# Last combining of the routed layer: VectorE held until the last result writes are issued, ScalarE scales half of the first choices

## The chip, the cores and the metric

The kernel runs on one core of one Trainium2 chip. The metric is the device time of one execution in microseconds (us); lower is better.

## The reference

Four layers follow each other on an activation x of 4 batches x 1024 positions x 128 features, each as x = x + layer(layernorm(x)): linear attention with decay, a mixture of 8 experts, a state-space layer, and a second mixture of experts ("routed"). Only the last one's end is touched here. Cut to what matters:

```python
combine, dispatch = _top2_gating(x @ router_w, capacity)        # 8 experts, two choices for each token
expert_in  = einsum('nec,nh->ech', dispatch, x)
hmid       = silu(einsum('ech,ehf->ecf', expert_in, w1) + b1)
expert_out = einsum('ecf,efh->ech', hmid, w2) + b2
y   = einsum('nec,ech->nh', combine, expert_out)               # w_a * first choice + w_b * second choice
out = y + 0.1 * (silu(x @ sw1 + sb1) @ sw2 + sb2)
x   = x + out
```

## The kernel before, in words

Each engine has its own instruction stream; they wait for each other through semaphores. The 4096 tokens lie in SBUF as 8 chunks of 128 partitions x (4 batches x 128 features) in `xs`. The last phase, `routed_phase`, sorts the tokens into expert queues in device memory (`queue_in`) and works through 40 groups of 256 queue rows: SP loads a group (line 1245), TensorE turns it, multiplies by W1 (L1387) and W2 (L1399), ScalarE applies the gate (L1464), and VectorE adds the second bias into `outs` (`kept_of`, L1616).

GpSimd writes each group back to `results` in device memory, in the order of the tokens, with two indirect DMAs of 128 rows (L1306): 80 in all, each taking its row numbers from `target` in SBUF. Three groups may be in flight. Before issuing group t, and three times after the loop, GpSimd runs `all_landed` (L1279 to L1282): it waits until group t - 3 has landed and raises the semaphore `sent` with `pool.sem_inc` (L1282).

`results` has a half for the first choices and a half for the second ones. The expert queues hold the first choices ahead of the second ones, so SP can load the first half into `back[0]` (the buffer `XN`, L1251) before the loop over the groups is done: it waits for a number of groups computed from the data (L1249). The second half is loaded into `back[1]` (the buffer `XT`, L1256) only after all 40 groups have landed (L1252); chunk 4 to 7 of it wait for the landing of the chunk four before.

The last combining is `xs += w_a * back[0]` and then `xs += w_b * back[1]`, chunk by chunk:

- VectorE adds the first choices of all 8 chunks, four instructions a chunk, one for each batch because the weight is one number a partition and batch (`weighted`, L1634 to L1643). They are `scalar_tensor_tensor` on 128x128 (L1637), 32 in all; the last of each chunk raises `weighed`. They come right after the last `kept_of` in VectorE's stream and wait only for `first_in`.
- VectorE then adds the second choices of chunks 0, 2, 4 and 6 the same way (L1644 to L1647).
- ScalarE scales the second choices of chunks 1, 3, 5 and 7 in place (L1469 to L1474), and GpSimd adds them to `xs` in one 128x512 `tensor_tensor` a chunk (L1318), once `weighed` says that the chunk's first choices are in. These stand in GpSimd's stream behind the last `all_landed`.
- SP stores the chunks 0 to 7 in this order (L1259).

Of the kernel before, what the change touches and what calls it, by code (L numbers as in the profile page):

```python
# [8 lines left out]
ALU = mybir.AluOpType  # L9
ACT = mybir.ActivationFunctionType  # L10
AX = mybir.AxisListType

P = 128
BATCH, SEQ, D = 4, 1024, 128
CHUNKS = SEQ // P
WIDE = BATCH * P
# [11 lines left out]
def at(i, per_turn, k):  # L28

    return i * per_turn + k  # L30


def wide(ap, n=BATCH):
    return ap.rearrange("p (b f) -> p b f", b=n)
# [1137 lines left out]
def routed_phase(nc, xs, of, queue_in, results, out, routing, w1, w2, b1, b2, sw1, sw2, sb1, sb2):  # L1172
# [3 lines left out]
    with ExitStack() as ctx:  # L1176
# [17 lines left out]
        best, second, w_a, w_b = (S.sb(n, TILES) for n in ("best", "second", "w_a", "w_b"))  # L1194
# [12 lines left out]
        back = [XN, XT]  # L1207
# [3 lines left out]
        s = {n: S.sem(n) for n in ("spread shared_in late_in columns kept lg_mm lg_out chain expd exped masked prefix slots "  # L1211
                                   "s_hid s_act s_outp s_evac due dispatched sent "
                                   "e_turned e_cols rows_read e_hid e_act e_outp e_outs weighed scaled "
                                   "first_in combined combined_pool stored").split()}
        fetched = [S.sem(f"fetched{k}") for k in range(4)]
        written = [S.sem(f"written{k}") for k in range(IN_FLIGHT)]

# [44 lines left out]
        @block.gpsimd  # L1262
        def _(pool):
            front.inverse_deviation(pool)
            pool.memset(restart[:, :], 1.0).then_inc(s["spread"], 1)
            pool.wait_ge(s["spread"], 1)
            pool.memset(restart[:, :].rearrange("p (k n) -> p k n", n=TILES)[:, :, 0:1], 0.0).then_inc(s["spread"], 1)
            with pool.Fori(0, CHUNKS // 2) as i:
                for k in range(2):
                    pool.wait_ge(front.normal, at(i, 2, k + 1))  # L1270
                    pool.sem_inc(front.held, 1)
                    pool.tensor_copy(by_row(XN[:, bass.ds(i * 2 * BATCH * ROW + k * BATCH * ROW, BATCH * ROW)])[:, :, 0:D],
                                     wide(front.xn[k][:, :])).then_inc(s["kept"], 1)

            pool.wait_ge(s["kept"], CHUNKS)
            pool.wait_ge(s["slots"], 2)
            landed = [0] * IN_FLIGHT

            def all_landed(k, what):  # L1279

                pool.wait_ge(written[k], landed[k])
                pool.sem_inc(what, 1)  # L1282

            n = 0
            for choice in range(2):
                for b in range(BATCH):
                    for c in range(CHUNKS):
                        tile = c * BATCH + b
                        if n >= IN_FLIGHT:
                            all_landed(n % IN_FLIGHT, s["dispatched"])  # L1290
                        pool.indirect_dma_start(queue_in, bass.IndirectOffsetOnAxis(slot[:, n:n + 1], 0),  # L1291
                                                XN[:, tile * ROW:(tile + 1) * ROW], None,
                                                bounds_check=SLOTS - 1, oob_is_err=False
                                                ).then_inc(written[n % IN_FLIGHT], 16)
                        landed[n % IN_FLIGHT] += 16
                        n += 1
            for n in range(SCATTERS, SCATTERS + IN_FLIGHT):
                all_landed(n % IN_FLIGHT, s["dispatched"])

            for t in range(GROUPS_OUT):  # L1300
                if t >= IN_FLIGHT:
                    all_landed(t % IN_FLIGHT, s["sent"])
                pool.wait_ge(s["e_outs"], t + 1)
                for j in range(2):
                    n = t % KEPT_BACK * 2 + j
                    pool.indirect_dma_start(results, bass.IndirectOffsetOnAxis(target[:, n:n + 1], 0),  # L1306
                                            outs[t % KEPT_BACK][:, j * P:(j + 1) * P], None,
                                            bounds_check=2 * BATCH * SEQ - 1, oob_is_err=False
                                            ).then_inc(written[t % IN_FLIGHT], 16)
                landed[t % IN_FLIGHT] += 32  # L1310
            for t in range(GROUPS_OUT, GROUPS_OUT + IN_FLIGHT):
                all_landed(t % IN_FLIGHT, s["sent"])

            for c in range(1, CHUNKS, 2):
                xc_ = xs[:, c * WIDE:(c + 1) * WIDE]
                pool.wait_ge(s["scaled"], c // 2 + 1)
                pool.wait_ge(s["weighed"], c + 1)
                pool.tensor_tensor(xc_, xc_, back[1][:, c * WIDE:(c + 1) * WIDE], ALU.add).then_inc(s["combined_pool"], 1)  # L1318
# [104 lines left out]
        @block.scalar  # L1423
        def _(act):
            act.sem_inc(s["lg_mm"], 2)
            with act.Fori(0, CHUNKS // 2) as i:
                for k in range(2):
                    act.wait_ge(front.turned, at(i, 2, k + 1))
                    act.activation(XT[:, bass.ds(i * 2 * WIDE + k * WIDE, WIDE)], front.turn[k][:, :], ACT.Copy)
                    act.wait_ge(s["lg_mm"], at(i, 2, k + 1))  # L1430
                    act.activation(xc[k][:, :], front.turn[k][:, :], ACT.Copy).then_inc(s["columns"], 1)
            act.wait_ge(s["expd"], 1)
            act.activation(logits[:, :], logits[:, :], ACT.Exp).then_inc(s["exped"], 1)

            def shared_gate(c):
                for m in range(HB):
                    act.wait_ge(s["s_hid"], c * HB + m + 1)
                    act.activation(hT[c % 2][:, m * WIDE:(m + 1) * WIDE], banks[m][:, :], ACT.Silu,
                                   bias=SB1[:, m:m + 1]).then_inc(s["s_act"], 1)

            def shared_kept(c):
                act.wait_ge(s["s_outp"], c + 1)
                act.activation(shared[:, c * WIDE:(c + 1) * WIDE], outp[c % 2][:, :], ACT.Copy).then_inc(s["s_evac"], 1)  # L1443

            act.wait_ge(s["shared_in"], 16 * len(shared_loads))
            shared_gate(0)
            shared_kept(0)
            shared_gate(1)
            for c in range(1, CHUNKS):
                if c + 1 < CHUNKS:  # L1450
                    act.wait_ge(s["s_outp"], c)
                    shared_gate(c + 1)
                shared_kept(c)

            act.wait_ge(s["late_in"], 16 * len(late))
            for t in range(GROUPS_OUT):
                e = t % EXPERTS
                if t >= 2:
                    act.wait_ge(s["e_outp"], t - 1)
                for h in range(HB // 2):  # L1460
                    q = t * HB // 2 + h
                    act.wait_ge(s["e_hid"], q + 1)
                    for m in (2 * h, 2 * h + 1):
                        last = act.activation(hT[t % 2][:, m * GROUP:(m + 1) * GROUP],  # L1464
                                              banks[q % 4][:, (m % 2) * GROUP:(m % 2 + 1) * GROUP], ACT.Silu,
                                              bias=B1[:, e * HB + m:e * HB + m + 1])
                    last.then_inc(s["e_act"], 1)

            for c in range(1, CHUNKS, 2):  # L1469
                act.wait_ge(*second_in[c])  # L1470
                for b in range(BATCH):
                    yb = back[1][:, c * WIDE + b * P:c * WIDE + (b + 1) * P]
                    last = act.activation(yb, yb, ACT.Copy, scale=w_b[:, b * CHUNKS + c:b * CHUNKS + c + 1])
                last.then_inc(s["scaled"], 1)  # L1474

        @block.vector
        def _(dve):
# [156 lines left out]
            def weighted(back_, w, c):  # L1634
                for b in range(BATCH):
                    xb = xs[:, c * WIDE + b * P:c * WIDE + (b + 1) * P]
                    last = dve.scalar_tensor_tensor(xb, back_[:, c * WIDE + b * P:c * WIDE + (b + 1) * P],  # L1637
                                                    w[:, b * CHUNKS + c:b * CHUNKS + c + 1], xb, ALU.mult, ALU.add)
                return last

            dve.wait_ge(s["first_in"], 16 * CHUNKS)
            for c in range(CHUNKS):
                weighted(back[0], w_a, c).then_inc(s["weighed"], 1)  # L1643
            for c in range(0, CHUNKS, 2):  # L1644
                dve.wait_ge(*second_in[c])
# [739 lines left out]
```

## Time and profile before

| | us |
|---|---|
| median of the 3 runs | 1039.56 (1039.24 to 1043.19) |
| the profiled execution's own time | 1034.82 |
| its span in the trace | 1033.0 |
| TensorE busy | 881.3 |
| VectorE busy | 551.8 |
| GpSimd busy | 480.9 |
| ScalarE busy | 444.4 |

Times in the trace are from the span's start. Engines: PE is TensorE, DVE is VectorE, ACT is ScalarE, POOL is GpSimd, SP is SyncE, which only issues DMAs. A name with a q (POOLq, SPq) is the engine's sequencer, which decodes the stream and hands instructions on to the engine. L12 is line 12 of the kernel. The chain of work is followed back from the last instruction through whatever released each step.

### The profile page before, as it was taken

What the parts mean: (1) busy time and instruction counts of PE and PEld (TensorE: products, weight loads), DVE (VectorE), ACT (ScalarE), POOL (GpSimd) and SP (SyncE); (2) the same over time, 40 slices, a digit from 0 to 9 for tenths busy, and PEclk for the clock granted to TensorE, in tenths of its full rate; (3) what the DMA queues carried; (4) which work ended last, traced back from release to release, by engine and by line L of the source; (5) the groups of instructions that cost most, each with busy time, mean ns of one, the idle gap of its engine ahead of it and who ended that gap; (6) DMA issues with size and microseconds to landing.
All of it is one profiled execution on the core that took longest, in us unless ns stands there. A gap on an engine that the chain in (4) does not pass through costs nothing. (4 is left out here: it accounts for less than half of the span.)

```text
span 1033.0 us, 24706 instructions
## 1 busy us (share of the span) xinstructions
PE 881.3 (85%) x8764; PEld 748.8 (72%) x8764; DVE 551.8 (53%) x1629; ACT 444.4 (43%) x941; POOL 480.9 (47%) x501
## 2 busy tenths in 40 slices
PE   4999999999999832988577779999967999999990
PEld 1788777877787731877465569999865679999980
DVE  4665656566664543655448867445476813222225
ACT  5535354353543211545227757443415444444431
POOL 3234333434434443777766300015512376677764
PEclk9999999999999865999889999999997999999995
DMA  7778500000000002333150001000013023322235
GB/s 233 281 264 332 203 17 5 21 8 13 15 7 21 22 21 57 103 105 96 51 165 2 3 8 16 3 3 3 1 49 160 21 73 87 82 85 85 84 103 163
DMA packets 72918, 79.28 MB, mean 77 GB/s; under 512 B 14429, under 2 KB 56676, under 8 KB 72320
## 3 DMA queue, kind: packets, MB, share of 16 engines
q1 hardware_dynamic: 61744, 59.69, 18.2%
q0 software_dynamic: 9216, 16.84, 4.8%
q10 hardware_dynamic: 1872, 1.58, 0.5%
q8 instruction: 57, 0.93, 0.4%
q14 instruction: 29, 0.24, 0.1%
HBM read 32.46 MB, written 47.77 MB: 78 GB/s over the span
## 5 line engine op out<-in xcount | busy, mean ns | idle before, releaser
L436 POOL TENSOR_TENSOR attn_qd<-attn_qT,attn_qpow 128x512 f32<-128x512 f32 x32 | 54.4, 1701 | 153.9 <-DVE attn_qT L726 153.9
L1464 ACT ACTIVATE routed_hT<-routed_hid,routed_B 128x256 f32<-128x256 f32 x160 | 65.7, 470 | 81.1 <-PE routed_hid L1387 81.0
L1306 POOL DMA_INDIRECT results<-routed_outs,routed_target x80 | 83.2, 1040 | 29.9 <-issue 15.5
L1034 POOL DMA_INDIRECT mixed<-moe_outs,moe_target x80 | 77.8, 972 | 38.5 <-DVE moe_outs L1136 15.3
L1291 POOL DMA_INDIRECT queue_in<-routed_XN,routed_slot x64 | 63.2, 988 | 46.3 <-DVE routed_slot L1559 22.2
L1399 PE MATMUL routed_outp<-routed_W,routed_hT 128*128 128x128 f32 x640 | 77.8, 275 | 0.0
L1387 PE MATMUL routed_hid<-routed_cols,routed_W 128*128 128x256 f32 x320 | 75.8, 380 | 0.5 <-DVE routed_cols L1607 0.5
L1399 PEld LDWEIGHTS routed_outp<-routed_W,routed_hT 128*128 128x128 f32 x640 | 74.7, 192 | 0.1
L595 PE MATMUL attn_av<-attn_v,attn_a 128*128 128x65 f32 x512 | 64.4, 280 | 9.3 <-DVE attn_a L737 8.9
L595 PEld LDWEIGHTS attn_av<-attn_v,attn_a 128*128 128x128 f32 x512 | 61.6, 197 | 13.4 <-DVE attn_a L737 13.0
L426 POOL DMA_INDIRECT sorted_rows<-attn_sent_rows,attn_slot x56 | 55.8, 997 | 18.3 <-issue 14.3
L1387 PEld LDWEIGHTS routed_hid<-routed_cols,routed_W 128*128 128x128 f32 x320 | 57.7, 190 | 6.9 <-ACT routed_shared L1443 0.7
L307 ACT ACTIVATE attn_kd<-attn_turn,attn_kpow 128x256 f32<-128x256 f32 x56 | 23.5, 470 | 90.9 <-PE attn_turn L586 90.9
L1070 PE MATMUL moe_hid<-moe_cols,moe_w 128*128 128x256 f32 x164 | 46.3, 406 | 8.0 <-DVE moe_cols L1127 7.6
L1607 DVE COPY routed_cols<-routed_turn 128x256 f32<-128x256 f32 x40 | 17.0, 424 | 64.2 <-PE routed_turn L1375 64.1
L1836 POOL TENSOR_TENSOR xs<-xs,powers_BOUT 128x512 f32<-128x512 f32 x8 | 10.2, 1270 | 85.3 <-DVE xs L2265 85.3
L295 ACT ACTIVATE attn_v<-attn_proj 128x512 f32<-128x512 f32 x32 | 19.2, 600 | 68.0 <-PE attn_proj L508 68.0
L1616 DVE TENSOR_TENSOR routed_outs<-routed_outp,routed_B 128x256 f32<-128x256 f32 x40 | 17.0, 424 | 55.4 <-PE routed_outp L1399 55.4
L1865 PEld LDWEIGHTS ssm_pb<-powers_XB,powers_XC 64*64 64x64 f32 x640 | 25.0, 144 | 28.1 <-issue 21.0
L1080 PEld LDWEIGHTS moe_outp<-moe_w,moe_hT 128*128 128x128 f32 x320 | 41.4, 191 | 5.0 <-issue 3.3
L1080 PE MATMUL moe_outp<-moe_w,moe_hT 128*128 128x128 f32 x320 | 42.8, 277 | 1.1 <-ACT moe_hT L1108 0.9
L292 ACT ACTIVATE attn_e<-attn_proj 128x512 f32<-128x512 f32 x64 | 38.2, 597 | 10.5 <-PE attn_proj L502 9.1
(330 smaller groups left out, 2264.5 us busy)
## 6 DMA issues: line engine op xcount, KB each, us to landing
sorted_rows<-attn_vacant SPq DMA_DIRECT2D x8, 2080.0 KB, 7.4
moe_rows<-sorted_rows SPq DMA_DIRECT2D x44, 130.0 KB
queue_in<-attn_empty SPq DMA_DIRECT2D x8, 645.0 KB, 7.2
routed_rows<-queue_in SPq DMA_DIRECT2D x40, 129.0 KB, 2.3
results<-attn_zero SPq DMA_DIRECT2D x8, 512.0 KB, 7.9
ssm_turn_buf<-mixed SPq DMA_DIRECT2D x16, 256.0 KB, 3.8
routed_W<-m1w SPq DMA_DIRECT2D x2, 2048.0 KB, 10.4
xs<-x SPq DMA_DIRECT2D x8, 256.0 KB, 4.2
```

Of the source, the lines that this page charges most:

```text
L292: act.activation(e[k][:, :], proj[k][:, :], ACT.Exp)
L426: pool.indirect_dma_start(sorted_rows, bass.IndirectOffsetOnAxis(slots[:, n:n + 1], 0), copies[k][:, b * TAGGED:(b + 1) * TAGGED], None, b ...
L436: pool.tensor_tensor(wide(of_pair(qd, p)), wide(of_pair(qT, p)), qpow[:, p * P:(p + 1) * P].unsqueeze(1).to_broadcast([P, BATCH, P]), ALU. ...
L595: mm = pe.matmul(av[:, h * 512 + b * (DK + 1):h * 512 + (b + 1) * (DK + 1)], a[:, h * WIDE + b * P:h * WIDE + (b + 1) * P], v4[:, b, 2 * p ...
L1034: pool.indirect_dma_start(results, bass.IndirectOffsetOnAxis(target[:, n:n + 1], 0), outs[q][:, j * P:(j + 1) * P], None, bounds_check=2 * ...
L1070: mm = pe.matmul(hid[q % 2][:, m * GROUP:(m + 1) * GROUP], w1[q % 2][:, m * P:(m + 1) * P], cols[q % 2][:, :], start=True, stop=True)
L1080: mm = pe.matmul(outp[q % 2][:, j * P:(j + 1) * P], hT[q % 2][:, m * GROUP + j * P:m * GROUP + (j + 1) * P], w2[q % 2][:, m * P:(m + 1) * ...
L1291: pool.indirect_dma_start(queue_in, bass.IndirectOffsetOnAxis(slot[:, n:n + 1], 0), XN[:, tile * ROW:(tile + 1) * ROW], None, bounds_check ...
L1306: pool.indirect_dma_start(results, bass.IndirectOffsetOnAxis(target[:, n:n + 1], 0), outs[t % KEPT_BACK][:, j * P:(j + 1) * P], None, boun ...
L1387: mm = pe.matmul(banks[q % 4][:, (m % 2) * GROUP:(m % 2 + 1) * GROUP], W1[:, (e * HB + m) * P:(e * HB + m + 1) * P], cols[t % 2][:, :], st ...
L1399: mm = pe.matmul(outp[t % 2][:, j * P:(j + 1) * P], hT[t % 2][:, m * GROUP + j * P:m * GROUP + (j + 1) * P], W2[:, (e * HB + m) * P:(e * H ...
L1464: last = act.activation(hT[t % 2][:, m * GROUP:(m + 1) * GROUP], banks[q % 4][:, (m % 2) * GROUP:(m % 2 + 1) * GROUP], ACT.Silu, bias=B1[: ...
```

## The change

GpSimd raises a new semaphore, `all_begun`, once, behind the loop that issues the 80 result writes. VectorE waits for it before the first choices. ScalarE, which waits for `first_in` after its last gate, scales the first choices of chunks 0 to 3 in place (16 activations on 128x128) and raises `first_scaled` once a chunk. VectorE adds these four chunks with one `tensor_tensor` of 128x512 each in place of four `scalar_tensor_tensor`; chunks 4 to 7 are added as before. The order of the stages stays.

```diff
-                                   "first_in combined combined_pool stored").split()}
+                                   "first_in first_scaled all_begun combined combined_pool stored").split()}
...
                                             ).then_inc(written[t % IN_FLIGHT], 16)
                 landed[t % IN_FLIGHT] += 32
+            pool.sem_inc(s["all_begun"], 1)
             for t in range(GROUPS_OUT, GROUPS_OUT + IN_FLIGHT):
                 all_landed(t % IN_FLIGHT, s["sent"])
...
+            act.wait_ge(s["first_in"], 16 * CHUNKS)
+            for c in range(CHUNKS // 2):
+                for b in range(BATCH):
+                    tile = back[0][:, c * WIDE + b * P:c * WIDE + (b + 1) * P]
+                    last = act.activation(tile, tile, ACT.Copy, scale=w_a[:, b * CHUNKS + c:b * CHUNKS + c + 1])
+                last.then_inc(s["first_scaled"], 1)
             for c in range(1, CHUNKS, 2):
                 act.wait_ge(*second_in[c])
...
             dve.wait_ge(s["first_in"], 16 * CHUNKS)
-            for c in range(CHUNKS):
+            dve.wait_ge(s["all_begun"], 1)
+            for c in range(CHUNKS // 2):
+                dve.wait_ge(s["first_scaled"], c + 1)
+                chunk = slice(c * WIDE, (c + 1) * WIDE)
+                dve.tensor_tensor(xs[:, chunk], xs[:, chunk], back[0][:, chunk], ALU.add).then_inc(s["weighed"], 1)
+            for c in range(CHUNKS // 2, CHUNKS):
                 weighted(back[0], w_a, c).then_inc(s["weighed"], 1)
```

## Rows read from the trace of the kernel before

**Rows 1.** The page's head: the span and each engine's busy time, share, instructions

```profile
span 1033.0 us, 24706 instructions
PE 881.3 (85%) x8764; PEld 748.8 (72%) x8764; DVE 551.8 (53%) x1629; ACT 444.4 (43%) x941; POOL 480.9 (47%) x501
```

**Rows 2.** The chain of work at the end: start us, us, what

```profile
1005.48 0.44 DVE routed_outs L1616
1005.91 0.02 issue
1005.94 0.03 POOLq L1306
...
1006.98 0.02 POOLq L1282
...
1008.89 7.38 DMA results<-routed_outs,routed_target
...
1016.33 0.36 SPq L1256
...
1027.52 1.34 POOL xs L1318
```

**Rows 3.** Timeline, GpSimd, its last result writes

```profile
1004.89 0.97 POOL L1306 DMA_INDIRECT results<-routed_outs,routed_target  x1 [1.27 <-DVE routed_outs L1616]
1006.16 1.10 POOL L1306 DMA_INDIRECT results<-routed_outs,routed_target  x1 [0.30 <-DVE routed_outs L1616]
1007.57 1.01 POOL L1306 DMA_INDIRECT results<-routed_outs,routed_target  x1 [0.30 <-issue]
1008.89 6.26 POOL L1306 DMA_INDIRECT results<-routed_outs,routed_target  x1 [0.30 <-issue]
```

**Rows 4.** All result writes of the phase: ns min/median/max, and their landing

```profile
L1306 POOL DMA_INDIRECT results<-routed_outs,routed_target x80: 969/972/6257, 904.5 to 1008.9; - x80
DMA to landing us min/median/max: 2.1/2.2/5.0
```

**Rows 5.** VectorE's first choices: timeline, then the line's group

```profile
1005.82 8.48 DVE L1637 SCALAR_TENSOR_TENSOR xs<-routed_XN,routed_w_a,xs 128x128 f32<-128x128 f32 x32
...
L1637 DVE SCALAR_TENSOR_TENSOR xs<-routed_XN,routed_w_a,xs x32: 343/346/347, 1005.8 to 1014.0; 128x128 f32<-128x128 f32 x32
```

**Rows 6.** Timeline, first second-choice work of each engine, and SP's issues

```profile
1016.33 6.68 SPq L1256 DMA_DIRECT2D routed_XT<-results  x8
1019.20 1.14 DVE L1637 SCALAR_TENSOR_TENSOR xs<-routed_XT,routed_w_b,xs 128x128 f32<-128x128 f32 x4 [4.90 <-DMA routed_XT<-results]
1023.05 6.79 SPq L1259 DMA_DIRECT2D out<-xs  x8
```

**Rows 7.** Windows, the last 16 us: busy by engine, clock, DMA share, GB/s

```profile
1016.30:1032.60 16.30, 0.00 (x0) 0.00 (x0) 7.12 (x16) 5.11 (x16) 5.21 (x4) 0.50 0.89 257
```

**Rows 8.** GpSimd's sequencer: the moves ahead of two writes, the semaphore raises behind

```profile
L1306 POOLq MOVE  x1: 29/29/29, 1004.7 to 1004.7; - x1
...
L1282 POOLq EVENT_SEMAPHORE  x1: 17/17/17, 1005.2 to 1005.2; - x1
...
L1306 POOLq MOVE  x1: 29/29/29, 1006.5 to 1006.5; - x1
...
L1282 POOLq EVENT_SEMAPHORE  x1: 17/17/17, 1007.0 to 1007.0; - x1
```

**Rows 9.** ScalarE's last gates and its scaling; SP's loads of the first choices

```profile
1001.10 1.64 ACT L1464 ACTIVATE routed_hT<-routed_hid,routed_B 128x256 f32<-128x256 f32 x4 [1.87 <-PE routed_hid L1387]
...
1020.05 1.28 ACT L1473 ACTIVATE routed_XT<-routed_XT,routed_w_b 128x128 f32<-128x128 f32 x4 [17.31 <-DMA routed_XT<-results]
...
981.54 6.37 SPq L1251 DMA_DIRECT2D routed_XN<-results  x8
```

**Rows 10.** VectorE on 128x512: two back to back, and the group of it

```profile
549.08 1.41 DVE L2200 SCALAR_TENSOR_TENSOR ssm_big_b<-ssm_big_a,powers_CW,ssm_big_b 128x512 f32<-128x512 f32 x2
...
L2200 DVE SCALAR_TENSOR_TENSOR ssm_big_b<-ssm_big_a,powers_CW,ssm_big_b x48: 737/743/1758, 549.1 to 610.1; 128x512 f32<-128x512 f32 x48
```

**Rows 11.** Timeline, scatters of GpSimd beside 128x512 adds of VectorE

```profile
822.06 0.69 DVE L1596 TENSOR_TENSOR routed_shared<-routed_shared,routed_SB 128x512 f32<-128x512 f32 x1
...
822.55 1.05 POOL L1291 DMA_INDIRECT queue_in<-routed_XN,routed_slot  x1 [0.30 <-DMA queue_in<-routed_XN,routed_slot]
...
831.50 0.69 DVE L1596 TENSOR_TENSOR routed_shared<-routed_shared,routed_SB 128x512 f32<-128x512 f32 x1 [5.59 <-ACT routed_shared L1443]
...
831.57 1.47 POOL L1291 DMA_INDIRECT queue_in<-routed_XN,routed_slot  x1 [0.30 <-issue]
...
856.52 0.68 DVE L1596 TENSOR_TENSOR routed_shared<-routed_shared,routed_SB 128x512 f32<-128x512 f32 x1
...
856.86 1.19 POOL L1291 DMA_INDIRECT queue_in<-routed_XN,routed_slot  x1 [0.30 <-DMA queue_in<-routed_XN,routed_slot]
```

## The prediction, made before the changed kernel ran

> **What bounds the kernel now.** I read the page's head first: TensorE is busy 85% of the span and no other engine is over 53% [rows 1], so most of the kernel is TensorE's and the change touches none of that. The change lies in the last 28 us, so the second view is the chain of work there [rows 2]. The reader is to see one outsized piece: from 1008.89 the chain runs 7.38 us through a single result write, and only then, at 1016.33, does SP start to load the second choices. The third view is GpSimd's timeline [rows 3]: the three writes before took 0.97, 1.10 and 1.01 us on the engine, the last one 6.26. All 80 have a median of 972 ns and that maximum [rows 4]. So the last write alone lost 6.26 - 0.97 = 5.29 us, all on the path.
>
> What held it? VectorE's 32 first-choice instructions run without a gap from 1005.82 for 8.48 us, to 1014.30 [rows 5]; the write ended at 1008.89 + 6.26 = 1015.15, that is 0.85 us after VectorE's end, and a free write takes 0.97. It looks as though the write asked for something that VectorE did not give up until its run was over. The work that held it had time to spare: VectorE's next instruction came at 1019.20, after 4.90 us of waiting [rows 6].
>
> Behind the write the tail is rigid: loads from 1016.33, stores from 1023.05 [rows 6], the DMA engines 0.89 busy at 257 GB/s up to the last store [rows 7]. What the loads gain in start, the end gains, as long as VectorE, ScalarE and GpSimd are ready for the chunks.
>
> **When does VectorE start now?** The change asks it to wait for a semaphore raised behind the last issue in GpSimd's program. But GpSimd's sequencer runs ahead of its engine. For the last group the second move was at 1006.5 and the semaphore raise behind it at 1006.98 [rows 8, 2], while that group's writes began on the engine at 1007.57 and 1008.89 [rows 3]. One group earlier the same: move 1004.7, raise 1005.2 [rows 8], write 1006.16 [rows 3]. The new raise stands at just this place, so it fires at about 1006.98, with two writes yet to run. VectorE starts at 1007.1 (0.1 for the hand-over, my estimate: from the end of VectorE's last bias add at 1005.91 to GpSimd's sequencer the chain shows 0.03 [rows 2], and there are three waits to pass). It is delayed by 1.3 us and not kept off the last two writes.
>
> **ScalarE's part.** Its last gates end at 1001.10 + 1.64 = 1002.74; the first choices were issued from 981.54 for 6.37 us, long landed. Four scalings of 128x128 take 1.28 us, 16 take 4 x 1.28 = 5.1, so the chunks are ready at about 1004.0, 1005.3, 1006.6 and 1007.9 [rows 9]. VectorE asks for them at 1007.1, 1007.7, 1008.3 and 1008.9: cost nothing. Its next own work is at 1020.05 [rows 9], so nothing is queued behind it either. If the cover were gone, VectorE would follow at 1.28 a chunk; ready at 1007.9 this still hardly counts.
>
> **VectorE's part.** A 128x512 add of two SBUF inputs took 0.69 [rows 11]. Back to back, two 128x512 instructions took 1.41 where one is 0.743 [rows 10], so an overlap of 0.08; an add every 0.61. Four adds start at 1007.10, .71, 1008.32 and .93. The 16 remaining small ones come every 8.48/32 = 0.265 [rows 5], from 1009.54, and end at about 1013.85. Removed are 16 x 0.265 = 4.2 us, added 2.4; with the start 1.3 later VectorE is done 0.45 earlier than now. By itself this is worth nothing.
>
> **What a write loses to an add.** Three scatters began during such an add: 831.57 against an add at 831.50 took 1.47 (0.50 lost), 822.55 against 822.06 took 1.05 (0.08), 856.86 against 856.52 took 1.19 (0.22) [rows 11]. Beginning plus loss is in each case 0.56 or 0.57 after the add's start. So a write waits until 0.565 into a running add and then goes, if it goes at the first chance.
>
> **The sum.** The write of 1006.16 is now free: 0.97, to 1007.13, and the next starts 0.30 later, 1007.43 (bounds 1007.43 to 1007.57 as now). The add of 1007.10 holds it to 1007.67: 0.24 lost, done 1008.64. The last write starts at 1008.94 in the add of 1008.93, is held to 1009.50, and is done at 1010.47. Now it is 1015.15: 4.68 us earlier. Loads start at 1011.65. The first second-choice chunk arrives at 1019.20 - 4.68 = 1014.5, when VectorE has been free for 0.7 us; GpSimd's first add needs `weighed` 2, long raised. The stage shifts whole: 1034.82 - 4.68 = 1030.1 for an execution like the profiled one. The median shown is 4.74 above the profiled time, a spread that this trace cannot explain; the shift off it gives 1039.56 - 4.68 = **1034.9 us**, -0.45%. For the unknown, what a write loses in a run of adds, the ends are nothing (then 5.47, below) and the whole run, as the last write lost it now.
>
> **The rivals.**
>
> *The last write is starved again.* The writes at 1006.16 and 1007.57 got through between two of VectorE's instructions, with 0.13 and 0.04 lost; the one at 1008.89 missed some twenty chances [rows 3, 5]. I can't say from the trace what made the difference. For getting through: the last write now comes 1.8 us after VectorE's start, about where the lucky one of 1007.57 was (1.75), the unlucky one 3.07. Against: behind the add the small instructions follow as densely as before. If it misses, it ends 0.85 after VectorE's 1013.85, at 1014.70: 0.45 earlier than now, 1039.1. This is also the case in which the change does not do what it says.
>
> *Both last writes are starved (the slower side).* The write starting at 1007.43 falls 0.33 after VectorE's start. If that one misses every chance, it goes only near 1013.85 and ends at 1014.70; the last starts 0.30 later and takes 0.97: 1015.97, 0.82 later than now. Everything shifts by it: 1040.4. It decides where the first of the two is not let in between the adds. Against it are the three scatters, all let in at the first chance [rows 11], though those adds did not overlap.
>
> *Adds hold no write.* Then the writes run 1007.43 to 1008.40 and 1008.70 to 1009.67, 5.47 earlier: 1034.1. The small instructions begin at 1009.54, too late to matter. The three losses of rows 11 speak against. The Trainium skill, "SBUF — State Buffer", section "Who interferes with whom", would have it so: a `tensor_tensor` takes only the read side of the shared ports, while making descriptors needs the write side (marked there as inferred). The rows disagree for scatters that also fetch row numbers from SBUF.
>
> *The raise waits for the writes after all*, contrary to rows 8. Writes end at 1008.40 and 1009.67, VectorE starts at 1009.8 and ends at 1016.5; the second chunk-0 work slips from 1013.7 to 1016.5. SP would reach its first store at 1023.05 - 5.47 = 1017.6, just when that chunk is done: also about 1034.1.
>
> **How the numbers follow.** About 0.5% (5.2 us) is what a measurement of this kernel can tell from no change. Chances: forecast 0.54, last write starved 0.26, both starved 0.06, adds hold nothing 0.07, raise in order 0.03, something unseen 0.04. The forecast is 0.5 us short of the 0.5% line; the unexplained spread of the runs carries it over in about a third of cases (0.18), the two cases of 5.47 in some 0.07, and a stage where usual runs lose more than the profiled one adds 0.03: faster 0.28. Slower by over 0.5% needs something unseen: 0.03. The rest is 0.69. The range covers 1034.1 and 1040.4 with half a microsecond below: 1033.6 to 1040.4.
>
> **What would show it.** Right: `all_begun` raised about 1 us or more before the last write starts; VectorE's first add 0.1 after; the last two writes at about 1.2 and 1.5 us; last write's end to SP's first load 1.18; the tail unchanged in shape. The add of 128x512 at 0.69. Wrong: a last write of 4 us or more, ending 0.85 after VectorE; or VectorE waiting for `first_scaled`; or SP's stores waiting for chunk 0.

## The result, and the profile after

Over 22 runs each, the changed kernel has a median of 1031.1 us (1027.88 to 1036.26) and the kernel before 1035.72 (1034.16 to 1043.19): 4.62 us less. The ratio of the means is 0.995 with a 95% interval of 0.9936 to 0.9964; that of the medians is 0.9955. The 22 of the kernel before include the three runs that were shown with it. The forecast was a gain of 4.68 us and a time of 1034.9, range 1033.6 to 1040.4. The gain came as forecast; the time lies outside the range, because the three runs shown, with a median of 1039.56, were a base 3.84 us too high.

Timed executions fall into two groups some 5 us apart, which part between 340 and 640 us of the span (over 340 to 600 us TensorE was granted 0.87 of its clock in the profiled executions of both kernels here, and 0.83 or 0.84 in some of the experiments'), so all tails are counted from T, the end of VectorE's last bias add (1005.90 in the kernel before, 1006.83 in the changed one).

The page's head, the kernel changed (against [rows 1]):

```profile
span 1028.8 us, 24712 instructions
PE 883.3 (86%) x8764; PEld 749.9 (73%) x8764; DVE 551.7 (54%) x1617; ACT 449.5 (44%) x957; POOL 477.5 (46%) x501
```

The chain of work at the end, changed kernel: start us, us, what (against [rows 2]):

```profile
1007.90 0.02 POOLq L1311
...
1009.85 2.61 DMA results<-routed_outs,routed_target
...
1012.52 0.36 SPq L1256
```

The piece that was 7.38 us is now 2.61. L1311 is the new raise. Timeline of the changed kernel, GpSimd's last four result writes, then VectorE, ScalarE and SP (against [rows 3, 5, 6, 9]):

```profile
1005.82 0.97 POOL L1306 DMA_INDIRECT results<-routed_outs,routed_target  x1 [1.27 <-DVE routed_outs L1623]
1007.10 0.97 POOL L1306 DMA_INDIRECT results<-routed_outs,routed_target  x1 [0.30 <-DVE routed_outs L1623]
1008.37 1.17 POOL L1306 DMA_INDIRECT results<-routed_outs,routed_target  x1 [0.30 <-issue]
1009.85 1.50 POOL L1306 DMA_INDIRECT results<-routed_outs,routed_target  x1 [0.30 <-issue]
...
1006.41 0.42 DVE L1623 TENSOR_TENSOR routed_outs<-routed_outp,routed_B 128x256 f32<-128x256 f32 x1 [1.36 <-PE routed_outp L1400]
1008.00 2.50 DVE L1654 TENSOR_TENSOR xs<-xs,routed_XN 128x512 f32<-128x512 f32 x4 [1.17 <-POOLq L1311]
1010.42 4.29 DVE L1644 SCALAR_TENSOR_TENSOR xs<-routed_XN,routed_w_a,xs 128x128 f32<-128x128 f32 x16
1015.49 1.14 DVE L1644 SCALAR_TENSOR_TENSOR xs<-routed_XT,routed_w_b,xs 128x128 f32<-128x128 f32 x4 [0.78 <-DMA routed_XT<-results]
...
1003.57 4.77 ACT L1474 ACTIVATE routed_XN<-routed_XN,routed_w_a 128x128 f32<-128x128 f32 x16
...
1012.52 6.55 SPq L1256 DMA_DIRECT2D routed_XT<-results  x8
1019.12 6.88 SPq L1259 DMA_DIRECT2D out<-xs  x8
```

The reader is to see four things. The raise at 1007.90 comes 0.47 us before the second-last write starts and 1.95 before the last. VectorE's first add follows the raise by 0.10. The two writes that meet the adds take 1.17 and 1.50. VectorE still waits 0.78 us for the first second choices, so its later start cost nothing. The last write is done at 1009.85 + 1.50 = 1011.35, T + 4.51; before it was T + 9.24. The tail from T to the span's end is 21.9 us, before 27.1. A write is called starved here when it was held for over 5 us, past many ends of VectorE instructions.

### The profile page after: what moved, and what is told of

It reads as the page before. It is cut to its first block and busy times, and to the rows that moved or that the text cites. A ratio compares the mean times of both kernels' runs of the same rounds, so it can differ in the third digit from the quotient of the medians.

```text
span 1028.8 us, 24712 instructions
## 1 busy us (share of the span) xinstructions
PE 883.3 (86%) x8764; PEld 749.9 (73%) x8764; DVE 551.7 (54%) x1617; ACT 449.5 (44%) x957; POOL 477.5 (46%) x501
## 5 line engine op out<-in xcount | busy, mean ns | idle before, releaser
L1306 POOL DMA_INDIRECT results<-routed_outs,routed_target x80 | 78.5, 981 | 28.3 <-issue 16.6
L426 POOL DMA_INDIRECT sorted_rows<-attn_sent_rows,attn_slot x56 | 55.9, 998 | 18.3 <-issue 14.3
```

Source lines behind the costliest of these rows:

```text
L426: pool.indirect_dma_start(sorted_rows, bass.IndirectOffsetOnAxis(slots[:, n:n + 1], 0), copies[k][:, b * TAGGED:(b + 1) * TAGGED], None, b ...
```

## The experiments

All tails at a glance. "Last write done" and "tail" count from T; "held" is what each of the last writes took beyond 0.97 us. These three columns are of one profiled execution; the ratio is of timed runs against the kernel before on the same chip. The cuts of code leave out declarations of buffers and semaphores.

| version | last writes held, us | last write done | tail | ratio, 95% |
|---|---|---|---|---|
| before | 0.13, 0.04, **5.29** | T + 9.24 | 27.1 | |
| before, again | 0.12, **5.81**, 0 | T + 10.52 | 28.4 | |
| changed | 0.20, 0.53 | T + 4.51 | 21.9 | 0.995 (0.9936 to 0.9964) |
| changed, again | 0.20, 0.53 | T + 4.51 | 22.3 | |
| wait alone | 0, 0 | T + 3.78 | 21.7 | 0.9954 (0.9927 to 0.998) |
| scaling and wide adds alone | 0.21, 0.53, 0.04 | T + 4.56 | 22.5 | 0.9948 (0.9924 to 0.9972) |
| raise from the engine | 0, 0 | T + 3.79 | 23.2 | 0.9968 (0.9943 to 0.9994) |
| before, memset after each chunk | 0, 0.01, 0.05 | T + 4.02 | 21.8 | 0.9953 (0.9932 to 0.9975) |
| before, memset 128x64 ahead | 0, 0, 0.01 | T + 3.79 | 21.7 | 0.9972 (0.9948 to 0.9995) |
| the same, again | 0, 0, **5.52** | T + 9.31 | 27.0 | |
| before, memset 128x512 ahead | 0.29, 0.04, **5.55** | T + 9.66 | 27.1 | 0.9997 (0.9967 to 1.0026) |
| before, one input from PSUM | 0, 0, 0 | T + 4.06 | 21.4 | 0.9961 (0.9936 to 0.9985) |
| wait alone, memset ahead | 0.02, 0.04 | T + 3.84 | 21.8 | 0.9935 (0.9908 to 0.9963) |
| changed, memset ahead | 0.41, 0.53 | T + 4.73 | 22.8 | 0.9925 (0.9901 to 0.9948) |

### Which half of the change does it: the wait

```diff
--- the kernel before
+            pool.sem_inc(s["all_begun"], 1)
...
             dve.wait_ge(s["first_in"], 16 * CHUNKS)
+            dve.wait_ge(s["all_begun"], 1)
             for c in range(CHUNKS):
                 weighted(back[0], w_a, c).then_inc(s["weighed"], 1)
```

> The kernel before, with the raise of all_begun and VectorE's wait for it alone; the first choices stay 32 small instructions and ScalarE scales none of them. Times are counted from T, the end of VectorE's last bias add (before: last write's issue done at T + 9.24; changed kernel: T + 4.51). VectorE should start at T + 1.17 and end at T + 9.6. Theory (the gain is the shift of VectorE's start alone: the last write comes about 1.8 us after that start and is let in between two instructions, as the write 1.75 us after it was before): last write 0.97 to 1.15 us, done by T + 4.1, gain of the kernel 4.5 to 5.2 us, ratio to before 0.995 to 0.996. Rival (it is the small instructions that starve a write, and the wide adds that let it in): last write over 5 us, done at T + 10.5, time 1 us over before, ratio 1.001.

Timeline, the last two writes and VectorE:

```profile
1013.80 0.97 POOL L1306 DMA_INDIRECT results<-routed_outs,routed_target  x1 [0.30 <-issue]
1015.07 0.97 POOL L1306 DMA_INDIRECT results<-routed_outs,routed_target  x1 [0.30 <-issue]
...
1013.46 8.54 DVE L1638 SCALAR_TENSOR_TENSOR xs<-routed_XN,routed_w_a,xs 128x128 f32<-128x128 f32 x32 [1.19 <-POOLq L1311]
```

Both writes began inside the run of small instructions, 0.34 and 1.61 us after its start, and lost nothing. VectorE was done only at T + 9.7, with no room left before the second choices, and the tail was 21.7 all the same. The theory stands, with a ratio of 0.9954: a later start of VectorE is enough.

### The other half: scaling and wide adds without the wait

```diff
--- the changed kernel
             dve.wait_ge(s["first_in"], 16 * CHUNKS)
-            dve.wait_ge(s["all_begun"], 1)
```

> The changed kernel without VectorE's wait for all_begun: ScalarE scales half, VectorE starts with the four wide adds at T (the end of its last bias add) and reaches the 16 small instructions at T + 2.4, ends at T + 6.7. The last write starts at about T + 3.0 to 3.2, in the small instructions. Theory (what counts is how long VectorE's dense run has lasted when the write asks; 3 us after its start it is starved, as before): last write held to the end of the run, done at T + 7.5, gain 1.7 us, ratio 0.998. Rival (let in at the first chance): done at T + 4.1, gain 4.5 to 5.2, ratio 0.995 to 0.996, and the wait for all_begun is worth nothing.

```profile
1012.75 1.18 POOL L1306 DMA_INDIRECT results<-routed_outs,routed_target  x1 [0.30 <-DVE routed_outs L1623]
1014.24 1.50 POOL L1306 DMA_INDIRECT results<-routed_outs,routed_target  x1 [0.31 <-issue]
1016.05 1.01 POOL L1306 DMA_INDIRECT results<-routed_outs,routed_target  x1 [0.30 <-issue]
...
1012.41 2.48 DVE L1653 TENSOR_TENSOR xs<-xs,routed_XN 128x512 f32<-128x512 f32 x4
1014.82 4.28 DVE L1644 SCALAR_TENSOR_TENSOR xs<-routed_XN,routed_w_a,xs 128x128 f32<-128x128 f32 x16
```

The rival won: the last write came 3.64 us after VectorE's start and still lost only 0.04. Its ratio of 0.9948 agrees. So each half removes the stall alone, and it is not simply the length of VectorE's busy time that starves a write. But this write met the small instructions only 1.23 us after the first of them.

### A raise that really comes after the last write

```diff
--- the changed kernel
-            pool.sem_inc(s["all_begun"], 1)
+            pool.memset(bound_free[0:1, 0:1], 0.0).then_inc(s["all_begun"], 1)
```

> The changed kernel with all_begun raised by a tiny memset on GpSimd's engine in place of the sequencer's raise, so that it comes only when the last write has been issued by the engine. VectorE then starts at about T + 3.9 and ends at T + 10.7 (T: the end of its last bias add). Both last writes 0.97 us, the last done at T + 3.8, 0.7 earlier than in the changed kernel. Theory (VectorE's lateness is covered, since SP's first store can't go before T + 11.6 and chunk 0 is done at T + 11.8): gain over before 5.0 to 5.4 us, ratio 0.9945 to 0.995. Rival (VectorE, now 2.8 us later, holds up GpSimd's adds and the stores): gain 2 to 4 us, ratio 0.996 to 0.998.

```profile
1009.57 0.97 POOL L1307 DMA_INDIRECT results<-routed_outs,routed_target  x1 [0.30 <-issue]
1010.53 0.09 POOL L1312 MEMSET routed_begun_mark<- 1x1 f32 x1
1010.71 2.50 DVE L1655 TENSOR_TENSOR xs<-xs,routed_XN 128x512 f32<-128x512 f32 x4 [3.95 <-POOL routed_begun_mark L1312]
...
1017.33 3.23 DVE L1645 SCALAR_TENSOR_TENSOR xs<-routed_XT,routed_w_b,xs 128x128 f32<-128x128 f32 x12
...
1011.72 6.41 SPq L1257 DMA_DIRECT2D routed_XT<-results  x8
1018.48 8.26 SPq L1260 DMA_DIRECT2D out<-xs  x8
```

(`bound_free` is a buffer of one element a partition, `begun_mark` in the trace.) The writes are as free as can be, SP loads from T + 4.96, and the tail of 23.2 us is 1.3 longer than in the changed kernel, 0.9 longer than in its second profile. VectorE turns to the second choices without a wait and late; the stores take SP 8.26 us in place of 6.88. The lateness is not covered, as the rival had it. This rests on one profile: the ratio, 0.9968, is on the rival's side, but its interval and that of the changed kernel overlap. It also shows the two kinds of raise side by side: the sequencer's comes 1.95 us before the last write starts, the engine's after its end.

### What opens the door: short breaks, small shifts

```diff
--- the kernel before, memset after each chunk
                 weighted(back[0], w_a, c).then_inc(s["weighed"], 1)
+                dve.memset(pause[:, c * P:(c + 1) * P], 0.0)
--- the kernel before, memset ahead (128x64, and 128x512 in a second version)
             dve.wait_ge(s["first_in"], 16 * CHUNKS)
+            dve.memset(pause[:, :], 0.0)
             for c in range(CHUNKS):
```

> The kernel before with one memset of 128x128 in VectorE's stream after the four first-choice instructions of each chunk (8 in all, some 0.2 us each, nothing reads them); no wait and no scaling by ScalarE. Theory (an instruction without a second SBUF input lets the waiting write in): the last write, 3 us into VectorE's run, waits at most for the rest of one chunk, so it takes 1.0 to 2.0 us, done by T + 5, gain 4 to 5 us, ratio 0.995 to 0.996. Rival (what holds the write is any busy VectorE, or chance, not the shape of its instructions): over 5 us, done 0.85 after VectorE's end at T + 10, ratio 1.000 to 1.001.

> The kernel before, unchanged, profiled once more. In four kernels with another order or start of VectorE's work the last write was let in; this asks whether its starving is a property of the kernel before or of the one profiled execution. Theory (a property: nearly every timed run of before is some 5 us over the others): last write again 6.0 to 6.5 us, done 0.85 after VectorE's end. Rival (chance): last write 0.97 to 1.2 us, and the tail after T (the end of VectorE's last bias add) 21.7 to 22 us in place of 27.1.

> The kernel before with one memset of 128x64 (about 0.1 us) ahead of VectorE's 32 small instructions, so that the last write asks about 3.0 us into the run in place of 3.07. Theory A (a fine matter of phase between write and instruction): let in, last write under 1.3 us, ratio 0.995. Theory B (what decides is how long or how many instructions the dense run has lasted, 12 of them): starved as before, over 5.5 us, ratio 1.000.

> The same with a memset of 128x512 (0.3 to 0.6 us), so that the last write asks 2.5 to 2.8 us into the run. Theory A (phase): either outcome, independent of the one above. Theory B (length of the run: let in at 1.6 and 1.75, starved at 3.07): between; if starved here and above, the bound lies below 2.8; if let in here and starved above, above 2.5.

> The kernel before with the memset of 128x64 once more: not one write lost anything in its profile, but most of its timed runs were like those of before. If the outcome is fixed by the program: again no loss, tail after T 21.7 us. If it differs from one execution to the next: at least one write held, perhaps one over 5 us, tail 27 us.

With a memset after every fourth instruction the last write (1014.63, 1.02 us) lost 0.05. The kernel before, profiled again, starved a write again, but the first of the last group and not the second:

```profile
1007.85 1.09 POOL L1306 DMA_INDIRECT results<-routed_outs,routed_target  x1 [0.30 <-issue]
1009.25 6.79 POOL L1306 DMA_INDIRECT results<-routed_outs,routed_target  x1 [0.30 <-issue]
1016.34 0.97 POOL L1306 DMA_INDIRECT results<-routed_outs,routed_target  x1 [0.30 <-issue]
...
1006.71 8.48 DVE L1637 SCALAR_TENSOR_TENSOR xs<-routed_XN,routed_w_a,xs 128x128 f32<-128x128 f32 x32
```

The memset of 128x64 gave two profiles of one program. In the first no write was starved (last one at 1015.04, 0.98 us, VectorE's run from 1012.22), in the second:

```profile
1009.30 6.49 POOL L1307 DMA_INDIRECT results<-routed_outs,routed_target  x1 [0.30 <-issue]
...
1006.48 8.47 DVE L1638 SCALAR_TENSOR_TENSOR xs<-routed_XN,routed_w_a,xs 128x128 f32<-128x128 f32 x32
```

The outcome is not fixed by the program, nor by the place alone: the two writes began 2.82 us into the run both times, 0.203 and 0.207 after the start of an instruction. Its total time does not tell the outcomes apart (1035.77 in the first profile, 1035.35 in the second), its time beside the granted clock does. The first profile, without a starved write, had a mean granted clock of 0.941. Seven more of the ten timed runs had 0.937 to 0.942 and took 1034.95 to 1037.04, where the kernel before took 1037.6 to 1041.38 on the same chip at such clocks; the other two, at 0.945 and 0.947, took 1029.15 and 1029.66, where it took 1033.78 to 1039.1. By this none of the ten had a starved write, and the ratio of 0.9972 understates what the memset gave, since eight of its ten runs but only ten of the 25 beside it were granted the lower clock. The longer memset left the last write starved (1014.74, 6.52 us, run from 1012.06) and the time at 0.9997; by its clocks one of its ten runs was free (1029.22 at 0.947). So a small delay is no dependable remedy, though one length of it nearly was.

The longer memset's 0.29 us is a different loss: the write at 1011.86 began 0.21 after the memset did, ahead of the run, and was let in at about the memset's end. That is one case, but a memset reads nothing, and in the kernel before an earlier scatter (L426, at 137.92) lost 0.27 with no VectorE instruction beside it: VectorE's inputs in SBUF are not all that can hold such a DMA.

What sets the starved writes apart is where in an unbroken run of small instructions they come. Of the writes that an instruction of such a run held at all, those that began within 1.8 us of its first one were let in after at most 0.13 us, in nine cases of nine: at 0.34 and 1.75 in the kernel before, at 1.14, 1.37 and 1.23 in its second profile, the longer memset and the wide adds alone, at 0.08 and 1.37 in the wait alone with a memset (below), and twice in the runs of four that memsets break up (0.01 and 0.05 lost). Of those from 2.5 us on, four of five were starved to the run's end: at 3.07, 2.54, 2.68 and 2.82, with one let through at 2.82. That is a pattern in these profiles; its cause is not shown. Early in a run the place in the instruction does not matter for it: four writes that began 0.18 after an instruction's start were let in at 1.23 to 1.75. Late in a run it may: the three that came at 0.18 were all starved, and of the two that came at 0.20 and 0.21, in the program whose timed runs show no starving, one was. Nearly every timed run of the kernel before seems to hold a starved write: of 76 taken beside the experiments, one alone (1028.37) lies 5 us and more below all the others.

### Is it the two inputs in SBUF

```diff
--- the kernel before
-                weighted(back[0], w_a, c).then_inc(s["weighed"], 1)
+                for b in range(BATCH):
+                    xb = xs[:, c * WIDE + b * P:c * WIDE + (b + 1) * P]
+                    last = dve.scalar_tensor_tensor(xb, back[0][:, c * WIDE + b * P:c * WIDE + (b + 1) * P],
+                                                    w_a[:, b * CHUNKS + c:b * CHUNKS + c + 1], front.turn[0][:, 0:P],
+                                                    ALU.mult, ALU.add)
+                last.then_inc(s["weighed"], 1)
```

> The kernel before with the second tensor input of the 32 first-choice instructions taken from a PSUM bank in place of xs (so the output leaves out the layer's input, the shared part and what was summed before, and takes in what lies in that bank); count, density and place stay. Theory (two inputs in SBUF are what keeps the write out): last three writes 0.97 us each, no loss at all, the last done at T + 3.8, ratio 0.9945 to 0.9955. Rival (any dense run on VectorE keeps it out, or the write side of the ports does): last write over 5 us, ratio 1.000.

```profile
1007.91 0.97 POOL L1306 DMA_INDIRECT results<-routed_outs,routed_target  x1 [0.30 <-issue]
1009.18 0.97 POOL L1306 DMA_INDIRECT results<-routed_outs,routed_target  x1 [0.30 <-issue]
...
1006.01 8.35 DVE L1645 SCALAR_TENSOR_TENSOR xs<-routed_XN,routed_w_a,routed_turn 128x128 f32<-128x128 f32 x32
```

A run as dense and as long, and the write at 1009.18, 3.17 us into it, takes 0.97. The three writes began 0.11, 0.09 and 0.08 after the start of an instruction. With both inputs in SBUF the place of 0.09 cost 0.12 and that of 0.08 only 0.02, so two of the three tell. It is one profile, in which no write met the place of 0.18 where the starved ones began; the ratio of 0.9961, with VectorE no less busy, agrees.

The traces hold a larger comparison. VectorE's bias adds have one input in PSUM too. The second profile of the kernel before has such a pair, a write that began 0.21 into a bias add and lost nothing:

```profile
1006.37 0.42 DVE L1616 TENSOR_TENSOR routed_outs<-routed_outp,routed_B 128x256 f32<-128x256 f32 x1 [1.36 <-PE routed_outp L1399]
1006.58 0.97 POOL L1306 DMA_INDIRECT results<-routed_outs,routed_target  x1 [0.30 <-issue]
```

In the 14 traces 174 writes began in a bias add, at any point of it, and the most that one lost was 0.01. The `tensor_tensor` of the same size with both inputs in SBUF (`routed_rest`) was met by one scatter in each trace, 0.24 or 0.25 after its start, and each of the 14 lost 0.05 to 0.07. So it is the second input in SBUF by which these instructions hold a write. That a run of them starves one for the same reason is the natural reading, shown by the one profile above.

### Does the changed kernel owe it to luck

```diff
--- wait alone, and the changed kernel; pause is 128x256
             dve.wait_ge(s["all_begun"], 1)
+            dve.memset(pause[:, :], 0.0)
```

> The kernel with only the wait for all_begun (32 small instructions, the run in which no write lost anything), plus one memset of 128x256 ahead of them, which should start the run about 0.2 us later. Theory, from the runs so far (a small instruction keeps a write out from about 0.08 to 0.22 us after its start, out of a period of 0.2625; a write let in at 0.22 puts the next one at 0.183 into an instruction; starving was seen only there, in 3 of 6): the first write in the run, which began 0.34 after the run's start, now begins 0.14 after it and loses 0.08; the last begins 0.18 into an instruction and either loses 0.04 or is starved to the end of the run, 8 us. Timed runs: somewhat slower than without the memset, a part of them by 5 to 6 us. Rival (the wait for all_begun protects the writes whatever the phase): no loss above 0.1 us, ratio 0.995.

> The changed kernel with the same memset of 128x256 ahead of the wide adds. Theory (a write held by a wide add is let in 0.565 after that add's start; adds come every 0.605, writes 1.275 after one another, so the last one always meets a wide add too and the small instructions come too late): the write in the first add loses 0.4 (0.2 in the changed kernel), the last one 0.53 again, done about T + 4.7, no starving, ratio 0.9955. Rival (the adds are let through by luck as well): a last write of more than 4 us.

> The changed kernel once more. If its two losses follow from the places of write and add, they are the same: 0.20 and 0.53 us, the last write done at T + 4.5, the tail after T (the end of VectorE's last bias add) 22.0 us. If they are chance: other losses, or a starved write.

Changed kernel with the memset ahead, then the changed kernel again:

```profile
1013.32 1.39 POOL L1307 DMA_INDIRECT results<-routed_outs,routed_target  x1 [0.30 <-issue]
1015.00 1.50 POOL L1307 DMA_INDIRECT results<-routed_outs,routed_target  x1 [0.30 <-issue]
...
1013.23 2.43 DVE L1656 TENSOR_TENSOR xs<-xs,routed_XN 128x512 f32<-128x512 f32 x4
```

```profile
1008.44 1.17 POOL L1306 DMA_INDIRECT results<-routed_outs,routed_target  x1 [0.30 <-issue]
1009.92 1.50 POOL L1306 DMA_INDIRECT results<-routed_outs,routed_target  x1 [0.30 <-issue]
```

The losses follow from the places: 0.20 and 0.53 twice, 0.41 and 0.53 with the shift, where 0.4 and 0.53 were expected. With the wait alone and the memset both writes were held for a moment (1.01 us at 1009.64, in a run from 1008.27), 0.02 and 0.04, and none starved; the theory had given starving an even chance there, and its timed runs, 0.9935, show none of it either. So at this early point of the run the place decides the small losses and does not bring on starving. That the wait protects by bringing the last write to within 1.4 to 1.8 us of VectorE's start is what the pattern above says; why that helps is not shown. No version was measurably faster than the changed kernel: the intervals overlap.

## Why the prediction was right, and where it was wrong

- **The raise runs ahead of GpSimd's engine.** Right: foreseen at T + 1.08, measured T + 1.07; VectorE from T + 1.17 (foreseen T + 1.2).
- **ScalarE's part costs nothing.** Right: 16 scalings in 4.77 us, done at 1008.34, and VectorE's only wait in front of the adds is for L1311.
- **VectorE's part.** Right: four adds in 2.50 us, all done at 1014.70, T + 7.87 (foreseen T + 7.95), with 0.78 us to spare.
- **What an add costs a write.** Right: 0.20 and 0.53 against 0.24 and 0.56. The issue was done at T + 4.51 against T + 4.57, 4.73 us earlier than before (foreseen 4.68). The Trainium skill's inference ("SBUF — State Buffer", section "Who interferes with whom"), by which a `tensor_tensor` would not hold the making of descriptors, does not carry over to these writes, which lost 0.20 and 0.53; they also take their row numbers from SBUF, and no run here separates that reading from the making of descriptors. Its statement that the second SBUF input is what goes through the shared side agrees with the PSUM experiment, 0 us lost.
- **The stage shifts whole.** Right to half a microsecond: the tail shrank by 5.17, SP's loads came 4.74 earlier. Of the 0.43 between, 0.12 lies between SP's first load and its first store and 0.31 behind it; the second profile of the changed kernel, with loads from the same place, has a tail 0.37 longer, so this is within what one execution differs from the next.
- **The rivals.** "The last write is starved again" did not happen in three profiles of the changed form. The argument for it being let in (1.8 us after VectorE's start, like the one at 1.75) turned out to be the pattern of all the profiles, but the prediction had no cause for it and gave it 0.54: that part was a bet that came out. That the first write of the last group can be the one starved was seen, but in the kernel before. "Adds hold no write" fell, and so did "the raise waits for the writes after all": it was raised 1.95 before the last.
- **The step that failed is the base.** "The shift off it gives 1039.56 - 4.68": three runs were taken for the kernel's time, although their median stood 4.74 above the profiled execution and the text itself could not explain it. Over 22 runs the kernel before has 1035.72, 0.90 above its profiled 1034.82; of the 76 taken beside the experiments 22 took 1039.24 or more, as all three had. Why all three did is open. From there the same shift gives 1031.04, and 1031.1 was measured. The range went with the base: its low end had to reach the profiled time less the shift, 1030.1.
- **The chances.** A gain just short of the 0.5% line was forecast (0.45%), with most of the chance there. The medians give 0.45%, the ratio 0.995 lies on the line.

What stays open: why a write that comes 2.5 us or more into the run misses twenty openings, whether it is time or the number of instructions that counts, and what part the place in the instruction has in it.

## What to carry to other kernels

Look for an indirect DMA on GpSimd whose issue ends 0.85 us after the end of an unbroken run of VectorE instructions with two SBUF inputs. What cured it here was letting VectorE start 1.3 us later, four wide adds in place of the first sixteen instructions, a break in the run after every four, or one input in PSUM, and it is worth what waits for the landing. A semaphore raised by GpSimd's sequencer says that work was handed over, not that it was begun; here that was soon enough, and with a raise that waits for the engine the tail was 0.9 to 1.3 us longer in its one profile. Take the base of a forecast from as many runs as the answer will be measured with, and where a few runs stand apart from the profiled execution, keep both in the range.

## What the runs showed of the hardware that was not expected

- One result write of the kernel before was starved in each of its two profiles, a different one each time, for 5.29 and 5.81 us, past some twenty ends of instructions at any of which others were let in.
- Whether it happens can differ between two executions of one program: 0.98 and 6.49 us for the same write, which began 2.82 us into the run both times.
- An add of 128x512 with both inputs in SBUF, 0.69 us long, holds a write that begins in it up to about 0.57 after the add's start: beginning at 0.37 (1008.37 in the add of 1008.00) the write lost 0.20. In the 14 traces 88 indirect DMAs began 0.02 to 0.54 into such an instruction, and all were held, none beyond 0.57. With a shorter instruction, of 128x128, the hold ended 0.22 after its start of 0.35 (0.04 lost by a write that began 0.18 after it); writes that began before 0.08 or after 0.22 lost nothing.
- With one input in PSUM the hold is gone: at most 0.01 us lost by 174 writes that began in a bias add of 128x256, against 0.05 to 0.07 for 14 of 14 scatters that met one of the same size with both inputs in SBUF.
